# The first projections with the next tile's additions and statistics ahead of this tile's parts, and two gathers ahead of each scale

## The reference

```python
x = x + 0.5 * L0_ffn(layernorm(x))     # mixture of experts, top 4 of 16, and a shared part
x = x + L0_attn(layernorm(x))          # 16 heads of 16, causal, with biases
x = x + 0.5 * L0_ffn(layernorm(x))
x = x + 0.5 * L1_ffn(layernorm(x))     # weights by table: w = lut[idx], 16 entries
x = x + L1_attn(layernorm(x))          # causal, no biases
x = x + 0.5 * L1_ffn(layernorm(x))
# L1_ffn: silu(x @ lut[gate_idx].T) * (x @ lut[up_idx].T) @ lut[down_idx].T, 688 x 256 each
# layernorm: (x - mean) / sqrt(var + 1e-5)
```

## Time and profile before

| | us |
| --- | --- |
| median of 3 runs | 2943.07 |
| lowest and highest | 2940.93, 2944.93 |
| the profiled execution's own time | 2951.69 |
| its span | 2949.9 |
| PE busy | 2494.3 (85%) |
| DVE busy | 1960.6 (66%) |
| ACT busy | 1449.6 (49%) |
| POOL busy | 1084.0 (37%) |
| POOL L97, 128 indirect DMAs of the first projections | 138.2, 1079 ns each |
| PE L411, 416 look-up matmuls | 115.8, 438 ns each |

### The profile page before, as it was taken

One profiled execution on the slowest core, in us unless ns is written; L12 is line 12 of the kernel. 1 busy time (PEld: TensorE's weight loads), 2 busy tenths in 40 slices (PEclk: granted clock), 3 DMA queues, 4 the chain that ended last, 5 costly groups with the idle time before them and its releaser, 6 DMA issues. The chain is left out here.

```text
span 2949.9 us, 49366 instructions
## 1 busy us (share of the span) xinstructions
PE 2494.3 (85%) x15174; PEld 1620.2 (55%) x15190; DVE 1960.6 (66%) x5524; ACT 1449.6 (49%) x3366; POOL 1084.0 (37%) x1556
## 2 busy tenths in 40 slices
PE   7775996687899999968877994788788999997998
PEld 5664996355433333346657993566572333334776
DVE  5654886555688878756656884555468888884444
ACT  3332554223358778734334552333464888774433
POOL 4563444564522223315563445553023222321000
PEclk9897998898889999979888996999897999998999
DMA  3434555454634544443335554232255355434000
GB/s 116 147 130 127 180 179 178 128 151 144 162 71 85 114 102 93 100 144 122 136 134 160 178 177 150 79 99 65 84 179 105 75 110 109 102 98 155 29 29 29
DMA packets 251508, 350.78 MB, mean 119 GB/s; under 512 B 42437, under 2 KB 200694, under 8 KB 245110
## 3 DMA queue, kind: packets, MB, share of 16 engines
q1 hardware_dynamic: 212854, 242.71, 31.4%
q0 software_dynamic: 38400, 104.91, 10.2%
HBM read 196.80 MB, written 149.92 MB: 118 GB/s over the span
## 5 line engine op out<-in xcount | busy, mean ns | idle before, releaser
L1288 DVE CUSTOM_DVE_ANT_0 attn_heads_masked_s<-attn_heads_s_ps,attn_heads_causal 128x768 bf16<-128x768 f32 (+7 forms) x1024 | 726.7, 754 | 137.1 <-PE attn_heads_s_ps L1090 125.6
L1207 ACT ACTIVATE attn_heads_probs<-attn_heads_st_ps 128x512 f32<-128x512 f32 (+3 forms) x1536 | 663.3, 494 | 233.1 <-PE attn_heads_st_ps L1109 219.4
L1125 PE MATMUL attn_heads_o_ps<-attn_heads_probs,attn_v_sb 128*32 128x512 f32 (+3 forms) x3072 | 328.6, 500 | 1.4 <-POOL attn_heads_probs L1032 1.3
L1598 POOL DMA_INDIRECT xs_dram<-moe_route_xn,rows_at x256 | 254.9, 996 | 191.8 <-DVE rows_at L1866 119.8
L1032 POOL TENSOR_SCALAR_AFFINE_SELECT attn_heads_probs<-attn_heads_probs 128x512 f32<-128x512 f32 x256 | 163.4, 638 | 363.2 <-ACT attn_heads_probs L1207 358.0
L1109 PE MATMUL attn_heads_st_ps<-attn_heads_more_st 99*128 99x512 bf16 x960 | 261.2, 329 | 0.1
L1090 PE MATMUL attn_heads_s_ps<-attn_heads_more_st 96*128 96x512 bf16 (+1 forms) x960 | 246.9, 335 | 10.7 <-DMA attn_heads_more_st<-k_dram 5.7
L2094 POOL DMA_DIRECT2D ys_dram<-moe_expert_y_sb x288 | 158.0, 549 | 243.9 <-DVE moe_expert_y_sb L2212 243.8
L1109 PEld LDWEIGHTS attn_heads_st_ps<-attn_heads_more_st 99*128 99x128 bf16 x960 | 84.4, 97 | 212.3 <-ACT attn_heads_probs L1207 158.3
L2126 PE MATMUL moe_expert_gu_ps<-moe_w_hi,moe_expert_xT_hi 128*128 x576 | 189.2, 328 | 1.9 <-DVE moe_expert_xT_lo L2194 1.9
L1090 PE MATMUL attn_heads_s_ps<-attn_stack 96*128 96x512 bf16 (+2 forms) x576 | 157.3, 358 | 22.0 <-DVE attn_heads_row_max L1288 10.9
(11 more groups left out here) (276 smaller groups left out, 6167.0 us busy)
## 6 DMA issues: line engine op xcount, KB each, us to landing
moe_expert_x_sb<-xs_dram SPq DMA_DIRECT2D x288, 128.0 KB, 2.0
ys_dram<-moe_expert_y_sb POOLq DMA_DIRECT2D x288, 128.0 KB, 2.1
o_dram<-attn_heads_oT SPq DMA_DIRECT2D x64, 256.0 KB, 3.8
moe_route_w_raw<-in_L_ffn_we_dram SPq DMA_DIRECT2D x96, 128.0 KB
q_dram<-attn_proj_parts SPq DMA_DIRECT2D x32, 384.0 KB, 2.7
k_dram<-attn_proj_parts SPq DMA_DIRECT2D x32, 384.0 KB, 2.9
x_mid<-moe_route_x_sb SPq DMA_DIRECT2D x16, 512.0 KB
attn_v_sb<-o_dram SPq DMA_DIRECT2D x32, 256.0 KB
```

The lines of the kernel that those rows point to most:

```text
L1125: last = pe.matmul(o_ps[h * VW:(h + 1) * VW, use % OB, TILE - w:TILE], v_sb[:, at:at + VW], probs[:, G % NR, h, 0:w], start=(j == 0), stop ...
L1207: act.activation(probs[:, G % NR, h, 0:w], st_ps[:, v % NB, 0:w], ACT.Exp, scale=scale)\
L1288: dve.tensor_tensor_reduce(out=masked_s[:, use % 4, 0:w], in0=s_banks[:, at * TILE:at * TILE + w], in1=causal[:, SEQ - w:SEQ], scale=1.0, ...
L1598: pool.indirect_dma_start(xs_dram, bass.IndirectOffsetOnAxis(rows_at[:, n * SUB + s, k:k + 1], 0), xn[:, n % RX, s, :], None).then_inc(sca ...
```

## The change

SyncE issues the table's row and the first index chunk ahead of x0 and the projection weights. ScalarE reads the index chunks between its other first instructions, and normalises tile t + 1 ahead of the parts of tile t. TensorE transposes half of tile 0 ahead of the last quarter of piece 1. VectorE orders its start anew, and does the additions of tile t + 1, its statistics and the first two quarters of masks ahead of the parts of tile t; the other two quarters stand behind the third split of output 2. GpSimd issues, from tile 1 on, two gathers ahead of each scale in place of one, here and in the first table layer, where the additions in tile 0 also move one chunk ahead.

```diff
--- before.py
+++ after.py
@@ -281,12 +281,12 @@
                     sp.wait_ge(found_ready, piece + 1)
                     sp.dma_start(w_dram[:, piece * TILE:(piece + 1) * TILE], found[:, piece % 2, :]).then_inc(found_stored[piece % 2], 16)
 
+                if lookup:
+                    sp.dma_start(lut_row[:, :], lut.rearrange("(a n) -> a n", a=1).to_broadcast([P, LUT])).then_inc(lut_loaded, 16)
+                    load_idx(0)
                 load_x(0)
                 for n, w in enumerate(w_qkv):
                     sp.dma_start(w_raw[:, n, :, :], w.rearrange("(k p) o -> p k o", p=P)).then_inc(w_loaded, 16)
-                if lookup:
-                    sp.dma_start(lut_row[:, :], lut.rearrange("(a n) -> a n", a=1).to_broadcast([P, LUT])).then_inc(lut_loaded, 16)
-                    load_idx(0)
                 for t in range(1, RX):
                     load_x(t)
                 if biased:
@@ -350,11 +350,13 @@
                     for u in range(SUB):
                         gather(u)
                 for t in range(TILES):
+                    ahead = 2 if t else 1
                     if combine and t + 1 < TILES:
-                        gather((t + 1) * SUB)
+                        for s in range(ahead):
+                            gather((t + 1) * SUB + s)
                     rstd_of(t)
                     if combine and t + 1 < TILES:
-                        for s in range(1, SUB):
+                        for s in range(ahead, SUB):
                             gather((t + 1) * SUB + s)
                 pool.memset(pads[:, :, HD:VW], 0.0).then_inc(ones_ready, 1)
                 pool.wait_ge(ones_ready, 1)
@@ -418,10 +420,13 @@
 
                 if lookup:
                     pe.wait_ge(diag_ready, LUT // 4)
-                    for piece in range(2):
-                        for quarter in range(4):
-                            look_up(piece, quarter)
+                    for quarter in range(4):
+                        look_up(0, quarter)
+                    for quarter in range(3):
+                        look_up(1, quarter)
                 x_turn(0, 0)
+                if lookup:
+                    look_up(1, 3)
                 x_turn(0, 1)
                 pe.wait_ge(w_ready, 3)
                 if biased:
@@ -491,24 +496,31 @@
                         act.wait_ge(found_stored[piece % 2], 16 * (piece // 2))
                     act.activation(found[:, piece % 2, :], w_ps[:, :], ACT.Copy).then_inc(found_ready, 1)
 
+                if lookup:
+                    read_idx(0)
                 for n in range(3):
                     act.wait_ge(w_loaded, 48)
                     act.activation(in_order(w_hi, n), by_dim(w_raw, n), ACT.Copy).then_inc(w_hi_ready, 1)
+                if lookup:
+                    read_idx(1)
                 if biased:
                     act.wait_ge(b_loaded, 80)
                     act.activation(bv_parts[:, 0, :], bv_row[:, :], ACT.Copy).then_inc(bv_hi_ready, 1)
                 if lookup:
-                    for c in range(CHUNKS):
-                        read_idx(c)
                     copy_found(0)
+                    read_idx(2)
                 normalise(0)
                 x_hi(0, 0)
                 x_hi(0, 1)
                 if lookup:
                     copy_found(1)
+                    for c in range(3, CHUNKS):
+                        read_idx(c)
                 if not combine:
                     normalise(1)
                 for t in range(TILES):
+                    if combine and t + 1 < TILES:
+                        normalise(t + 1)
                     first(t, 0)
                     first(t, 1)
                     second(t, 0)
@@ -528,7 +540,6 @@
                     if not combine:
                         continue
                     if t + 1 < TILES:
-                        normalise(t + 1)
                         for kd in range(KD):
                             x_hi(t + 1, kd)
                     if lookup and t + 2 < PIECES:
@@ -607,18 +618,27 @@
                                           ALU.mult).then_inc(diag_ready, 1)
                 if not combine:
                     find_moments(0)
+                if lookup:
+                    masks(0, 0)
+                    masks(0, 1)
                 for n in range(3):
                     dve.wait_ge(w_hi_ready, n + 1)
                     dve.tensor_tensor(in_order(w_lo, n), by_dim(w_raw, n), in_order(w_hi, n).bitcast(F32), ALU.subtract)\
                         .then_inc(w_ready, 1)
-                for half in range(2):
-                    if lookup:
-                        for quarter in range(4):
-                            masks(half, quarter)
-                    if combine:
-                        combine_rows(0, half)
+                if lookup:
+                    masks(0, 2)
+                    masks(0, 3)
                 if combine:
+                    combine_rows(0, 0)
+                if lookup:
+                    masks(1, 0)
+                    masks(1, 1)
+                if combine:
+                    combine_rows(0, 1)
                     find_moments(0)
+                if lookup:
+                    masks(1, 2)
+                    masks(1, 3)
                 if biased:
                     dve.memset(ones[:, :].bitcast(F32), 1.0)
                     dve.wait_ge(bv_hi_ready, 1)
@@ -626,13 +646,15 @@
                        .then_inc(bv_ready, 1)
                 x_lo(0, 0)
                 x_lo(0, 1)
-                if combine:
-                    combine_rows(1, 0)
-                some_masks(0, 0)
-                some_masks(0, 1)
                 if not combine:
                     find_moments(1)
                 for t in range(TILES):
+                    if combine and t + 1 < TILES:
+                        combine_rows(t + 1, 0)
+                        some_masks(t, 0)
+                        some_masks(t, 1)
+                        combine_rows(t + 1, 1)
+                        find_moments(t + 1)
                     take_first(t, 0)
                     take_first(t, 1)
                     third(t, 0)
@@ -646,23 +668,12 @@
                     third(t, 2)
                     if not combine and t + 2 < TILES:
                         find_moments(t + 2)
+                    some_masks(t, 2)
+                    some_masks(t, 3)
                     third(t, 3)
-                    if not combine:
-                        continue
-                    if t + 1 < TILES:
-                        if combine:
-                            combine_rows(t + 1, 1)
-                        find_moments(t + 1)
-                        some_masks(t, 2)
-                        some_masks(t, 3)
+                    if combine and t + 1 < TILES:
                         for kd in range(KD):
                             x_lo(t + 1, kd)
-                    if t + 2 < TILES:
-                        if combine:
-                            combine_rows(t + 2, 0)
-                    if t + 1 < TILES:
-                        some_masks(t + 1, 0)
-                        some_masks(t + 1, 1)
 
         before.give_way(used)
 
@@ -2245,7 +2256,7 @@
     RAW = 3
     GAIN = 0.5
 
-    COMBINE_AT = ((2, 3), (0, 1))
+    COMBINE_AT = ((1, 2), (0, 1))
     TURN = turns_of_tiles(inputs_first=False)
     upper, lower = slice(0, HALF), slice(HALF, P)
 
```

## The result

The changed kernel took 2905.06 us in the median of 4 runs (2895.85 to 2909.48) beside 2944.0 for the kernel before: ratio 0.9856, 95% interval [0.9818, 0.9894], so 39 us or 1.4% faster. The forecast was 17 us. The direction was right in this comparison, and the gain was more than twice the forecast. The profiled execution took 2908.34 us, span 2906.6, against 2951.69 and 2949.9.

What follows compares the result with a forecast made beforehand. It took a per-tile loop through four engines to bound the first projections: -22.0 there, +3 late signals, +1.7 first table layer make -17.3, from 2943.07 to about 2926 us; range 2908 to 2946 with the rivals.

Steps and rivals of the forecast that it cites:

- The start of the stage: First projections: with the table's row issued first, look-ups start at 511.7 and tile 0's first projection matmul at 544.1, 13.7 earlier.
- A steady tile: First projections, tiles with gathers: period of 30.9 us against 32.8, bounds 29.0 to 32.8.
- F: First projections: when the next tile's rows are normalised, put 17.8 us after the current tile's first projection matmul.
- The term for the last tile: First projections, last tile, without gathers: 26.2 us, from 9.15 + 4.0 + 13.1.
- T_7: Start of tile 7's first projection matmul: forecast 761.3 against 783.31, 22.0 us less.
- The late signals: First projections: TensorE's results seen late by ScalarE, 7.6 us in one tile; after the change 3 us in all.
- the gathers, not VectorE, end last, by 4.6 us: Steady tile of the first projections: eight gathers end at 13.8 us after its first matmul, moments ready at 9.15.
- The first table layer: The second gather ahead of each scale costs the first tile 1.7 us (between 1.4 and 4); steady tiles cost nothing.
- Rival B: Shorter gather bursts end the late signals; steady table-layer tiles gain about 2 us each, six times: 2911, chance 0.20.
- two hit in each: First projections: two gathers stretched beside masks in each burst of eight, forecast about 1.9 x 5 us higher.
- the likeliest's own range: Whole kernel, main forecast (chance 0.45): 2916 to 2937, from periods of 29.0 to 32.8 and the start two us either side.
- Rival D: First projections: late signals on every tile, period 36.0 us, whole +10.3 or 2953, chance 0.12.

Runs made afterwards that it cites:

- e14: The kernel before itself, unchanged, run and profiled in a later group where nothing was late: 2816.75 us.
- e4: The changed kernel with one gather ahead of each scale again in the first projections only: 2873.36 us, ratio to before 0.9864.
- e2: The changed kernel with one gather ahead of each scale again in the first table layer only: ratio to before 0.999.
- e7: The changed kernel with masks of quarters 0 and 1 behind the next tile's statistics in place of between the additions: ratio to before 0.9898.
- e3: The kernel before with two small GpSimd powers between the eighth and ninth of twelve gathers in the first table layer: ratio 0.9942.
- e11: The kernel before with gathered rows of 512 bytes in place of 1 KB in both stages: ratio 0.9988.
- e15: The kernel before with gathered rows of 512 bytes in both stages, a repeat of e11 in another group: ratio 0.9986.
- e12: The kernel before with 2.1 us of GpSimd powers behind the sixth of twelve gathers in the first table layer: ratio 1.002.
- e16: e12 once more, in another group: ratio 1.0021.
- e18: The changed kernel with one gather ahead of each scale and a 2.1 us break behind the sixth of twelve, in both stages: ratio to before 0.9967.
- e20: The same kernel as e18, run once more: ratio to before 0.996.
- e5: The kernel before with one small GpSimd addition between the sixth and seventh of twelve gathers in the first table layer: ratio 1.0013.
- e1: The kernel before with only two gathers ahead of each scale in place of one in the first table layer: ratio 0.9923.

## Why the prediction was wrong

**The start of the stage** was right. In the changed profile the last expert matmul came 2.3 us later (493.3 in place of 491.0), so the forecast 511.7, 544.1 and 580.6 are to be read as 514.0, 546.4 and 582.9. Measured are 514.08, 545.28 and 581.52.

**A steady tile** was right in its order and 1.6 us short: 32.5 against 30.9. F came at T + 19.1 (730.34 on 711.20) and not at T + 17.8, because two gathers of the eight were stretched and took 3.5 more, not one that took 1.9. Both are inside the stated bounds; the sum used the nearer row. The term for the last tile was 1.9 too long (24.34 against 26.2). The stage ended 3.3 us worse than "all as now" said: from T_7 to the heads 16.2 in place of 13.0. The last store of a weight piece went out at 777.88 and the heads began 6.9 behind it, in place of 3.6 behind 792.66.

**The late signals** in the first projections: I had put +3 behind the change and found none. What I did not see was their size before. I took tile 6, whose part came after 3.9, as a tile without them; a part that is not late comes after 1.8, so tile 6 had lost 2.1 and tile 5 had lost 9.7, not 7.6. With nothing late the same code has a period of 27.5 (e14), not 32.8. So the step "the gathers, not VectorE, end last, by 4.6 us" described a loss, 14 to 16 us over the stage (e4), and the late signals that went with it paid for it. Their sum came out as -17.1 from the last expert matmul to T_7 against the forecast's -22.0 + 3.

**The first table layer** is the step that failed: "Its rows are taken by ScalarE as xT_hi at 1931.58 only, over 10 us after; steady tiles cost nothing." The distance from the normalised rows to 1931.58 was read as room. 4.7 us of it were the late half, with TensorE idle for 6.14 behind it, and this bounded every tile from 2 to 6. Rival B had the mechanism (the signal comes with the end of the burst, and eight gathers in place of twelve end sooner) but a price of 2 us per tile, taken from nothing but bounds; the timeline of TensorE around 1931 showed 6.14. The price is 6.1 per tile (34.0 to 27.9), 32.7 in the layer between these two profiles; 18 in the group of e2 and e4.

**The stretched gathers**: they took 2.56 beside masks, 2.87 beside additions and 4.11 in e7, each ending 0.8 after VectorE's run. The rule of the Trainium skill quoted in the forecast ("SBUF — State Buffer", section "SBUF: two separate sides") agrees with the one beside the masks, if the masks are such two-port operations, which no run here shows. For instructions with two inputs in SBUF, as the additions are, the same section has the lock only against a GpSimd operation that reads SBUF, and no run here shows whether the issue of a gather is one. The variant "two hit in each" that I worked out beside it had the right count. Not every gather beside such a run is held: one of the kernel before takes 0.95 at 722.19 beside additions from 720.20 to 723.45, and what tells these cases apart stays open.

**Of the range and the chances**: the sum gives 2914 and not 2916 for the lower end of the likeliest's own range, since 9.5 for the periods and 2 for T_0 belong below 2926 as they do above it. The direction was luck in part, since it hung on the group in which the comparison was run. Rival D, slower, is what happens where nothing is late (1.0078), though by another path than D named; it came from the eight gathers ahead of the scale, not from late parts.

**Open** is what holds TensorE's signals back. Shown are that it was met only in stages in which GpSimd issues indirect DMAs, that a held half comes in a pause of them (e3), that in the table layer it came with the eighth gather behind a scale, and that in four groups of runs it did not come at all. Whether the bytes of the gathers matter (e11, e15) and whether the break behind the sixth helps the table layer (e12, e16, e18, e20) was only run where nothing is late. The six groups of experiments ran on six different chips (late signals on two, none on four), and no chip was used twice, so whether it belongs to the chip or to something else that differs between the groups stays open. So does the recording: every time here comes with a recorded span and clock, records were lost in just the stages that grew, and no run without recording is at hand. And since the ends of matmuls are modelled, a signal held back and transposes that end late can't be told apart.

## What to carry to other kernels

A distance between a producer and its consumer is slack only if the engine between them is busy: look at what TensorE does in it, and if it idles with no releaser, that idle time, with the slower clock behind it, is about the price of whatever ends it. An order that starves one engine (eight gathers ahead of a scale that needs none of them) can still win because it breaks up a burst. Try a break in its place: with one gather ahead of the scale and a pause among the twelve behind it, the rest of the change won on both kinds of group (0.980 and 0.995), where with two gathers ahead it won 1.4% on one and lost 0.8% on the other. A break alone in the kernel before was tried only in the table layer, where with late signals it did less than the second gather (0.994 in e3 and 1.001 in e5, against 0.992 in e1). And run the kernel before once more beside each group: a gain of 39 us that turns into a loss of 22 can't be told from one comparison. Where two profiles of one kernel differ, count their records too: a loss in just the stages that grew means that the measuring may have a part in it.

## What the runs showed of the hardware

- One kernel took 2943, 2918 and 2818 us in the median in different groups. The 132 us between the spans 2949.9 and 2817.6 lie in the four stages in which GpSimd issues indirect DMAs (143 us there, the rest gave some back).
- With such DMAs running, in the first three groups alone, a signal of TensorE reached ScalarE up to 5.4 us late in the table layer (tile 1 of the kernel before, 6.0 in place of 0.6) and up to 10.0 in the first projections (tile 3, 11.8 in place of 1.8). In e3 it came within a 2 us pause of the issuing.
- In these groups 17 to 20% of the records of semaphores are missing beside the others, all in the stages with indirect DMAs.
- A gather of 128 rows takes 0.95 us of GpSimd at 512 bytes a row as at 1 KB (mean 1.03 and 1.04 us over 128 of them in the table layer, e15 and e14), so halving the bytes does not shorten a burst.
